# Layer 0 router weights: stored transposed in DRAM and spread over the rows of an expert pair by a DMA

## The chip, the core and the metric

The kernel runs on one core of a Trainium2 chip, as one launch. The metric is the device time in microseconds (us) of the whole launch. Five engines work side by side: TensorE (PE, with its weight loads as PEld), VectorE (DVE), ScalarE (ACT), GpSimd (POOL) and SyncE (SP), and DMA transfers are issued by an engine's queue and land later.

## The reference, cut to what matters

Two layers follow each other; each computes `x = x + s * silu(ffn(xn))`, where `s` is a recurrence (layer 0) or attention (layer 1). The change is in the mixture of experts of layer 0, with 64 experts of width 64, of which a token uses 8:

```python
def _gate(x, gate_w, gate_bias):                 # x: 4096 tokens x 128
    scores = jax.nn.sigmoid(x @ gate_w.T)
    ...                                          # best 4 of 8 groups, then best 8 experts
    tw = tw / (tw.sum(-1, keepdims=True) + 1e-20)
    return (tidx, tw * SCALE)
...
w_dense = jnp.zeros((T, E), tw.dtype).at[jnp.arange(T)[:, None], tidx].add(tw)
def body(acc, ws):
    wg, wu, wdn, cw = ws
    hmid = jax.nn.silu(x @ wg) * (x @ wu)
    return (acc + cw[:, None] * (hmid @ wdn), None)
```

The kernel computes all 64 experts for every token and multiplies the hidden values of each by its router weight `cw`, which is zero for the experts not chosen.

## The kernel before

Layer 0 (`layer0`) works on 8 tiles of 512 tokens (`NT` = 8, `TOK` = 512). Two pieces of work run beside each other for each tile `t`.

The first is the recurrence, on DVE: 32 steps of nine chained instructions (`step`, L756 to L771). Between the steps stand, at fixed places, pieces of the next tile's preparation (`between`): its layer norm at steps 3, 6, 7 and 12, its router (`route`, L643 to L697) after step 20, the key sums and coefficients of its recurrence at steps 23 to 27 (`coefficients`, the last one L726), and at steps 5 and 9 the output norm of the tile before (`out_sums`, L776, and `out_norm`, L780).

The second is the experts, in 32 pairs and one shared expert (`PAIRS + 1` = 33 rounds), a pipeline over three engines with the two experts of a pair side by side on the 128 partitions, 64 rows each:

- PE (`experts`) fills slots of a ring of four PSUM banks: the gate product and the up product of a pair (`split3`, L502 to L504), and as third slot the router weights of the pair, spread over its 128 rows by a product of a selector matrix `sel` with the transposed weights `cwt` (L583). It then does the down product of the pair two back (`down`, L554).
- ACT (`tile`, L481) copies each slot to SBUF, into the rings `act_g`, `act_u` and `act_c` of three pairs each. Before a pair's first copy it waits until the pair three back has been used (`s_h`).
- POOL (`tile`) multiplies `act_g` and `act_u` (L387) and then with `act_c` (L391), for the shared expert only once (L394). PE's down product takes the result.

At a tile's start PE transposes the router weights (L545) and ACT copies them to `cwt` (L459). At its end ACT copies the sum (L483), PE transposes it (L591), ACT applies silu (L485), and SP stores the gate to `g_scratch` (L267). At the top of pair 15 PE and ACT project the next tile (`project`); SP stores the result in 16 transfers to `z_scratch` (L260) and loads it back (L263). ACT takes it up at pair 22 (`recurrence_inputs`), POOL at pair 23 (`products`) and pair 29 (`vectors`, L327 to L340, which waits for the coefficients of DVE, L726). At pair 5 POOL does the gating of the recurrence's output of the tile before (`gated`, L345 to L352), which waits for the end of its 32 steps on DVE; DVE's `out_sums` at step 5 waits for it. SP stores the finished output at L271. Every order is written out by hand, and each engine executes its program in that order. Layer 1 starts when layer 0 is done.

The rows of the first tile's weights pass through the three rings as staging buffers; POOL splits them (L367, L369), and ACT's slots begin after the last split (`s_split`). All DMAs of the kernel before are issued by SP.

Of the kernel before, what the change touches and what calls it, by code (L numbers as in the profile page):

```python
# [7 lines left out]
F32 = mybir.dt.float32  # L8
# [6 lines left out]
P = 128  # L15
# [3 lines left out]
TOK = B * TP  # L19
# [18 lines left out]
NEG = -1e30  # L38
SLOTS = 3 * PAIRS + 2
STEPS = 9  # L40
# [20 lines left out]
def layer0(nc, d, scratch, sem):  # L61

    z_dram, y_dram, g_dram = scratch
    with ExitStack() as ctx:
# [4 lines left out]
        ident = sb("ident", [P, P])  # L69
        onehot = sb("onehot", [P, E0])  # L70
        tri = sb("tri", [P, G0 * G0])
# [12 lines left out]
        wd = sb("wd", [P, PAIRS + 1, D])  # L84
        sel = sb("sel", [P, E0, F0], F32R)
        x_sb = sb("x_sb", [P, NS, D])
# [16 lines left out]
        cw_sum = sb("cw_sum", [P, NS])  # L103
        cws = sb("cws", [P, NS, 2 * E0], F32R)
        cwt = sb("cwt", [P, TOK], F32R)
        RING = 3
        act_g = sb("act_g", [P, RING, TOK])
        act_u = sb("act_u", [P, RING, TOK])
        act_c = sb("act_c", [P, RING, TOK])
        hid1 = sb("hid1", [P, TOK])  # L110
# [25 lines left out]
        s_eps = sem("eps_set")  # L136
        s_sel = sem("selectors_ready")
        s_w1t_ps = sem("transposed_small_in_psum")
# [21 lines left out]
        s_rt = sem("router_chain")  # L160
        s_cws = sem("router_weights_split")
        s_cwt_ps = sem("router_weightsT_in_psum")
        s_cwt = sem("router_weightsT_ready")
        s_slot = sem("moe_slot_filled")
        s_ev = sem("moe_slot_copied")
# [22 lines left out]

        LN, PREP, POST, ROUTE = 3, 7, 4, 57
        RAW, WHOLE = 5, 14  # L190
# [15 lines left out]
        root, neg_beta, am_scale, square, along_k, q_am = (coef[:, i, :] for i in range(6))  # L206
        SMALL = 13

# [8 lines left out]
        def _(sp):  # L217
# [86 lines left out]
        def _(pool):  # L304
# [66 lines left out]
            def tile(t, par, first, ahead):  # L371
                for p in range(PAIRS + 1):
                    if not first and p == POST_PAIRS[0]:
                        gated(t - 1, 1 - par)
                    if not first and p == POST_PAIRS[1]:
                        normed(t - 1)
                    if ahead and p == PREP_PAIRS[0]:
                        products(t + 1, 1 - par)
                    if ahead and p == PREP_PAIRS[1]:
                        vectors(t + 1, 1 - par)  # L380

                    pool.wait_ge(s_ev, t * SLOTS + min(3 * p + 3, SLOTS))
                    g, u, c = act_g[:, p % RING, :], act_u[:, p % RING, :], act_c[:, p % RING, :]
# [21 lines left out]
        def _(act):  # L405
# [50 lines left out]
            def tile(t, par, first, ahead):  # L456

                act.wait_ge(s_cwt_ps, t + 1)
                act.activation(cwt[:, :], pb[:, 1, :], ACT.Copy).then_inc(s_cwt, 1)  # L459

                act.wait_ge(s_gst, t * 16)
                act.wait_ge(s_split, len(chunks) + 1)
                for r in range(SLOTS):
                    p, what = r // 3, r % 3
# [3 lines left out]
                    if ahead and r == 3 * PROJECT_PAIR:  # L468
# [30 lines left out]
        def _(pe):  # L499
# [38 lines left out]
            def experts(t, par, ahead):  # L538
                pe.wait_ge(s_cws, t + 1)
                pe.wait_ge(s_ev, t * SLOTS)  # L540
# [7 lines left out]
                pe.wait_ge(s_sel, 1)  # L548
                pe.wait_ge(s_wd, 32)
# [13 lines left out]
                for p in range(PAIRS + 1):  # L563
                    if ahead and p == PROJECT_PAIR:
                        pe.wait_ge(s_ev, t * SLOTS + 3 * p)
                        project(t + 1, 1 - par)
                        pe.wait_ge(s_zc, (t + 2) * NS)
                        pe.wait_ge(s_sc, t + 2)
                    pe.wait_ge(s_split, 2 * (2 * p // CH + 1))
                    for what, (w_hi, w_lo) in enumerate(((wg_hi, wg_lo), (wu_hi, wu_lo))):  # L570
                        r = 3 * p + what
                        slot_free(r)
# [29 lines left out]
        def _(dve):  # L602
# [37 lines left out]
            def route(t):  # L640
# [51 lines left out]
                dve.wait_ge(s_rt, c.next())  # L692
                dve.tensor_tensor(cw[:, :, :], cw[:, :, :], over(cw_sum[:, :], E0), ALU.mult).then_inc(s_rt, 1)
                dve.wait_ge(s_rt, c.next())
                dve.tensor_copy(cws[:, :, 0:E0], cw[:, :, :]).then_inc(s_rt, 1)
                dve.wait_ge(s_rt, c.next())
                dve.tensor_tensor(cws[:, :, E0:2 * E0], cw[:, :, :], cws[:, :, 0:E0].bitcast(F32), ALU.subtract).then_inc(s_cws, 1)  # L697
                c.check()
# [972 lines left out]
def build(nc, d, out):  # L1671
# [3 lines left out]

    z = scratch("z_scratch", NT, NS, BS, H0, TP, ZC)
    y = scratch("y_scratch", NT, P, TP, HD0)
    g0 = scratch("g0_scratch", NT, NS, P, D)
    x2 = scratch("x2_scratch", B, N, D)
    g1 = scratch("g1_scratch", B, N, D)  # L1680
    with ExitStack() as ctx:
        def sem(name):
            return ctx.enter_context(nc.semaphore(name))

        layer0(nc, d, (z, y, g0), sem)
        layer1(nc, d, (y, g0, x2, g1), out, sem)


def constants():
# [3 lines left out]
        "c_ident": np.eye(P, dtype=f),  # L1693
        "c_onehot": np.tile(np.eye(E0, dtype=f), (2, 1)),
        "c_tri": np.tril(np.ones((G0, G0), f), -1).reshape(-1),
# [48 lines left out]
```

## Time and profile before

| | |
|---|---|
| time, median of 3 runs | 2396.91 us (2391.91 to 2397.82) |
| profiled execution, its time | 2401.08 us |
| its span | 2399.3 us |
| mean granted TensorE clock | 0.882 of full speed |
| layer 0: experts' first slot copy, last store of the recurrence's output | 100.67 us, 1323.12 us |
| busy: PE, DVE, ACT, POOL | 77%, 67%, 45%, 38% of the span |

The times in the profile are counted from the start of the span. Layer 0 takes its first 1323 us, layer 1 the rest. A share of busy time is an average over both layers.

### The profile page before, as it was taken

The page shows a single profiled execution, that of the slowest core. Times are in us where ns is not written, and L with a number is a line of the kernel's source. Part 1 is how long each engine was busy: PE and PEld are TensorE (multiplying, and loading weights), DVE is VectorE, ACT ScalarE, POOL GpSimd, SP SyncE. Part 2 cuts the span into 40 slices and gives each one's busy share as a digit, 9 for nine tenths or more (in the row PEclk, how much of TensorE's full clock was granted, in tenths as well). Part 3 has the DMA queues.
Part 4 walks back from the last instruction along what each step waited for, and adds up shares of the span by engine and source line. Part 5 has one row for each costly group of instructions (what it writes and reads, how often), then busy time and mean ns, then how long its engine had stood idle before and what let it go on. Part 6 is the DMA issues. An engine that isn't in the chain of part 4 may idle for free. (4 is left out here: it accounts for less than half of the span.)

```text
span 2399.3 us, 35571 instructions
## 1 busy us (share of the span) xinstructions
PE 1837.1 (77%) x10242; PEld 1372.1 (57%) x10242; DVE 1615.1 (67%) x4233; ACT 1075.5 (45%) x1779; POOL 910.0 (38%) x729
## 2 busy tenths in 40 slices
PE   1384875866848768477486299898999999999998
PEld 1252553533525435244253288787888777777776
DVE  3599899898997989989989344444444444444443
ACT  2262553643625536355253155454455344444443
POOL 2776775757767667577486100000000000000000
PEclk8697887977978879789798599999999799999999
DMA  6220030200300203002000411111100100000000
GB/s 108 59 49 0 10 49 6 38 17 6 54 1 14 45 6 54 0 5 49 5 5 5 118 21 22 23 23 24 19 14 14 40 8 14 13 13 13 13 13 11
DMA packets 140839, 60.21 MB, mean 25 GB/s; under 512 B 94599, under 2 KB 135036, under 8 KB 140668
## 3 DMA queue, kind: packets, MB, share of 16 engines
q1 hardware_dynamic: 140668, 58.24, 12.0%
q8 instruction: 70, 1.15, 0.2%
q14 instruction: 101, 0.83, 0.1%
HBM read 37.10 MB, written 21.10 MB: 24 GB/s over the span
## 5 line engine op out<-in xcount | busy, mean ns | idle before, releaser
L554 PE MATMUL pb<-hid,wd 128*128 128x512 f32 x528 | 319.8, 691 | 215.6 <-POOL hid L391 211.0
L387 POOL TENSOR_TENSOR hid<-act_g,act_u 128x512 f32<-128x512 f32 x256 | 331.1, 1293 | 277.4 <-ACT act_c L481 260.1
L391 POOL TENSOR_TENSOR hid<-hid,act_c 128x512 f32<-128x512 f32 x256 | 332.7, 1300 | 20.1
L481 ACT ACTIVATE act_g<-pb 128x512 f32<-128x512 f32 (+1 forms) x264 | 158.5, 600 | 389.2 <-PE pb L504 386.1
L1239 PE MATMUL l_pb<-l_xt,l_big 128*128 128x512 f32 (+1 forms) x1024 | 299.4, 415 | 34.6 <-DVE l_rope L1518 24.1
L1586 DVE SCALAR_TENSOR_TENSOR l_acc<-l_pb,l_gtok,l_acc 128x128 f32<-128x128 f32 x512 | 144.0, 344 | 256.8 <-PE l_pb L1239 256.8
L502 PE MATMUL pb<-xt_hi,wg_hi 128*128 128x512 f32 (+1 forms) x264 | 223.9, 848 | 67.0 <-DMA wd<-in_L_ffn_Ws_down_dram 51.1
L554 PEld LDWEIGHTS pb<-hid,wd 128*128 128x128 f32 x528 | 96.6, 208 | 301.6 <-POOL hid L391 280.1
L1239 PEld LDWEIGHTS l_pb<-l_big,l_hid 128*128 128x128 f32 x2048 | 247.1, 192 | 10.6
L1628 DVE TENSOR_REDUCE l_mrow<-l_pb 128x2 f32<-128x256 f32 (+1 forms) x256 | 137.2, 556 | 171.9 <-PE l_pb L1239 168.9
L1167 ACT ACTIVATE l_hid<-l_pb,l_cols 128x512 f32<-128x512 f32 x256 | 169.4, 688 | 183.1 <-PE l_pb L1239 182.7
L1239 PE MATMUL l_pb<-l_big,l_hid 128*128 128x128 f32 x2048 | 247.9, 275 | 0.0
L1239 PEld LDWEIGHTS l_pb<-l_xt,l_big 128*128 128x128 f32 x1024 | 194.6, 200 | 73.0 <-DVE l_rope L1518 22.7
L756 DVE TENSOR_TENSOR products<-zr,rs 128x512 f32<-128x512 f32 x256 | 175.7, 686 | 23.7 <-POOL zr L340 10.4
L1204 ACT ACTIVATE l_big<-l_pb 128x768 f32<-128x768 f32 x128 | 104.6, 817 | 176.0 <-PE l_pb L1398 89.4
L502 PE MATMUL pb<-xt_hi,wu_hi 128*128 128x512 f32 (+1 forms) x264 | 116.3, 441 | 77.8 <-ACT act_g L481 77.7
L759 DVE TENSOR_REDUCE rs<-products 128x32 f32<-128x512 f32 x256 | 175.8, 687 | 0.0
L1105 POOL TENSOR_TENSOR l_ql<-l_rope,l_qh 128x512 f32 x8 | 10.3, 1289 | 434.5 <-ACT l_qh L1161 434.5
L757 DVE TENSOR_TENSOR products<-zr,rs 128x512 f32<-128x512 f32 x256 | 174.1, 680 | 0.0
L481 ACT ACTIVATE act_u<-pb 128x512 f32<-128x512 f32 (+1 forms) x264 | 158.1, 599 | 24.6 <-PE pb L504 16.5
L481 ACT ACTIVATE act_c<-pb 128x512 f32<-128x512 f32 x256 | 153.1, 598 | 0.0
L1239 PE MATMUL l_pb<-l_mT,l_esel 128*128 128x256 f32 x512 | 143.3, 280 | 0.0
(305 smaller groups left out, 4125.4 us busy)
## 6 DMA issues: line engine op xcount, KB each, us to landing
z_scratch<-zs SPq DMA_DIRECT2D x128, 81.0 KB, 4.2
zr<-z_scratch SPq DMA_DIRECT2D x8, 1296.0 KB, 8.4
x_sb<-in_L_attn_x_dram SPq DMA_DIRECT2D x32, 64.0 KB, 3.2
g_scratch<-act_u SPq DMA_DIRECT2D x8, 256.0 KB, 2.3
y_scratch<-yo SPq DMA_DIRECT2D x8, 256.0 KB, 2.3
l_xs<-in_L_attn_x_dram SPq DMA_DIRECT2D x32, 64.0 KB, 1.9
l_ys<-y_scratch SPq DMA_DIRECT2D x128, 16.0 KB, 1.7
l_gs<-g_scratch SPq DMA_DIRECT2D x8, 256.0 KB, 3.0
```

The lines of the kernel that those rows point to most:

```text
L387: pool.tensor_tensor(hid1[:, :], g, u, ALU.mult).then_inc(s_h1, 1)
L391: pool.tensor_tensor(hid[:, p % 2, :], hid1[:, :], c, ALU.mult).then_inc(s_h, 1)
L481: act.activation(dst, pb[0:n, r % 4, :], ACT.Silu if what == 0 else ACT.Copy).then_inc(s_ev, 1)
L502: pe.matmul(out, l_hi, r_hi, start=first, stop=False, skip_group_check=True)
L554: last = pe.matmul(pb[:, 4, :], wd[0:n, p, :], hid[0:n, p % 2, :], start=(p == 0), stop=(p == PAIRS), skip_group_check=True)
L756: dve.tensor_tensor(products[:, 2:4], two(ZG), twice, ALU.mult).then_inc(s_st, 1)
L757: dve.tensor_tensor(products[:, 0:2], two(ZF), twice, ALU.mult).then_inc(s_st, 1)
L759: dve.tensor_reduce(rs[:, 3, 0:2], products[:, 2:4], AX.X, ALU.add).then_inc(s_st, 1)
L1167: act.activation(hid[:, r % HR, :], pb[:, 2 + r % 3, :], ACT.Relu, bias=cols[:, r:r + 1]).then_inc(s_hid, 1)
L1239: return pe.matmul(out, l, r, start=start, stop=stop, skip_group_check=True)
L1586: dve.scalar_tensor_tensor(out=acc[:, s, :], in0=pb[:, 5 + e % 2, sub], scalar=gtok[par][:, s, e:e + 1], in1=acc[:, s, :], op0=ALU.mult, o ...
L1628: dve.tensor_reduce(mrow[:, k, 2 * j:2 * j + 2], src, AX.X, ALU.max).then_inc(s_ua_dve, 1)
```

## The change

Instead of a third PSUM slot for each pair, the transposed router weights go to DRAM once per tile (`c_scratch`, 64 experts x 512 tokens, two copies in turn), and for each pair a DMA issued by ACT reads the two experts' rows of it, each 64 times, into the 128 rows of `act_c`. It is issued two pairs ahead. The ring of `act_c` grows from three pairs to five. The weights are no longer split in two parts on DVE, the selector matrix and its constant are gone, and PE's transposition takes the unsplit weights. A pair now has two slots instead of three; the places of the other work, which are counted in slots, are renumbered so that they stay at the same pairs.

```diff
-SLOTS = 3 * PAIRS + 2
+SLOTS = 2 * PAIRS + 2
...
-        cws = sb("cws", [P, NS, 2 * E0], F32R)
-        cwt = sb("cwt", [P, TOK], F32R)
-        RING = 3
+        cwt = sb("cwt", [E0, TOK])
+        RING, CRING = 3, 5
...
-        act_c = sb("act_c", [P, RING, TOK])
+        act_c = sb("act_c", [P, CRING, TOK])
...
-        PROJECT_PAIR, NORM_SLOT, INPUT_SLOT = 15, 24, 66
-        POST_SLOT, KEY_SLOT = 30, 84
+        PROJECT_PAIR, NORM_SLOT, INPUT_SLOT = 15, 16, 44
+        POST_SLOT, KEY_SLOT = 20, 56
...
+        def spread(t, p):
+            per_tile = len(range(p % CRING, PAIRS, CRING))
+            return s_c[p % CRING], (t * per_tile + p // CRING + 1) * 16
...
-            sp.dma_start(onehot[:, :], d["c_onehot"]).then_inc(s_small, 16)
...
-                    pool.wait_ge(s_ev, t * SLOTS + min(3 * p + 3, SLOTS))
+                    pool.wait_ge(s_ev, t * SLOTS + 2 * p + 2)
...
                         pool.wait_ge(s_h1, t * PAIRS + (p + 1))
+                        pool.wait_ge(*spread(t, p))
...
-                act.activation(cwt[:, :], pb[:, 1, :], ACT.Copy).then_inc(s_cwt, 1)
+                act.activation(cwt[:, :], pb[0:E0, 1, :], ACT.Copy).then_inc(s_cwt, 1)
+
+                def load_weights(p):
+                    src = c_dram[par, 2 * p:2 * p + 2, :].unsqueeze(1).to_broadcast([2, F0, TOK])
+                    act.dma_start(act_c[:, p % CRING, :], src).then_inc(s_c[p % CRING], 16)
 
                 act.wait_ge(s_gst, t * 16)
                 act.wait_ge(s_split, len(chunks) + 1)
+                act.wait_ge(s_cwt, t + 1)
+                act.dma_start(c_dram[par], cwt[:, :]).then_inc(s_cst, 16)
+                act.wait_ge(s_cst, (t + 1) * 16)
+                load_weights(0)
+                load_weights(1)
...
                     if what == 0 and p >= RING:
                         act.wait_ge(s_h, t * (PAIRS + 1) + (p - RING + 1))
-                    dst = (act_g, act_u, act_c)[what][0:n, p % RING, :]
+                    if what == 0 and p + 2 < PAIRS:
+                        load_weights(p + 2)
+                    dst = (act_g, act_u)[what][0:n, p % RING, :]
...
-                    last = pe.transpose(pb[:, 1, P * s:P * (s + 1)], cws[:, s, :].bitcast(F32), ident[:, :])
+                    last = pe.matmul(pb[0:E0, 1, P * s:P * (s + 1)], cw[:, s, :], ident[:, :], start=(s == 0), stop=True, skip_group_check=True)
...
-                    if p < PAIRS:
-                        r = 3 * p + 2
-                        slot_free(r)
-                        pe.matmul(pb[:, r % 4, :], sel[:, 2 * p:2 * p + 2, :].rearrange("p a b -> p (a b)"), cwt[:, :], start=True, stop=True).then_inc(s_slot, 1)
...
-            dve.tensor_copy(sel[:, :, :], over(onehot[:, :], F0)).then_inc(s_sel, 1)
...
-                dve.tensor_copy(cws[:, :, 0:E0], cw[:, :, :]).then_inc(s_rt, 1)
-                dve.wait_ge(s_rt, c.next())
-                dve.tensor_tensor(cws[:, :, E0:2 * E0], cw[:, :, :], cws[:, :, 0:E0].bitcast(F32), ALU.subtract).then_inc(s_cws, 1)
...
+    c = scratch("c_scratch", 2, E0, TOK)
```

## Rows read from the trace of the kernel before

**Rows 1.** The page: busy us, share and instructions of each engine.

```profile
PE 1837.1 (77%) x10242; PEld 1372.1 (57%) x10242; DVE 1615.1 (67%) x4233; ACT 1075.5 (45%) x1779; POOL 910.0 (38%) x729
```

**Rows 2.** Waits up to 1400 us: who waited for whom, total, times, longest.

```profile
POOL zr L327 <- DVE coef L726: 72.5, 8, 9.9
DVE ynorm L776 <- POOL prod L352: 68.9, 8, 11.9
```

**Rows 3.** Timeline of POOL, PE, ACT and DVE around the change of tile.

```profile
694.90 0.20 DVE L726 TENSOR_TENSOR coef<-sums,coef 128x32 f32<-128x32 f32 x1
...
708.10 2.08 PE L554 MATMUL pb<-hid,wd 128*128 128x512 f32 x2 [18.05 <-POOL hid L391]
...
712.19 1.27 POOL L391 TENSOR_TENSOR hid<-hid,act_c 128x512 f32<-128x512 f32 x1
...
712.53 1.06 PE L554 MATMUL pb<-hid,wd 128*128 128x512 f32 x1
...
714.28 1.26 POOL L394 TENSOR_TENSOR hid<-act_g,act_u 64x512 f32<-64x512 f32 x1 [0.82 <-PE pb L554]
...
722.39 0.60 ACT L459 ACTIVATE cwt<-pb 128x512 fp32r<-128x512 f32 x1 [3.70 <-PE pb L545]
...
727.17 1.30 POOL L387 TENSOR_TENSOR hid<-act_g,act_u 128x512 f32<-128x512 f32 x1 [11.63 <-ACT act_c L481]
728.54 1.30 POOL L391 TENSOR_TENSOR hid<-hid,act_c 128x512 f32<-128x512 f32 x1
...
739.47 1.30 POOL L391 TENSOR_TENSOR hid<-hid,act_c 128x512 f32<-128x512 f32 x1
...
745.61 0.69 DVE L776 TENSOR_REDUCE ynorm<-prod 128x32 f32<-128x512 f32 x1 [11.93 <-POOL prod L352]
```

**Rows 4.** Timeline of DVE at the end of a tile's router.

```profile
663.69 1.24 DVE L695 CAST cws<-cw 128x256 fp32r<-128x256 f32 x1
664.96 1.44 DVE L697 TENSOR_TENSOR cws<-cw,cws 128x256 fp32r<-128x256 f32 x1
```

**Rows 5.** The instructions on line 583 and on line 481 to act_c.

```profile
L583 PE MATMUL pb<-cwt,sel x256: 388/397/632, 101.6 to 1289.8; 128*128 128x512 f32 x128
...
L481 ACT ACTIVATE act_c<-pb x256: 590/592/646, 102.9 to 1290.5; 128x512 f32<-128x512 f32 x128
```

**Rows 6.** DMA in 1339.8:1340.3, 453:454.2, 719.5:721.2, 91:97: packets, MB, busy share of 16 engines.

```profile
q1 hardware_dynamic: 2, 0.00, 0.2%
...
q1 hardware_dynamic: 144, 0.26, 58.2%
...
q1 hardware_dynamic: 528, 0.26, 48.2%
...
q1 hardware_dynamic: 880, 1.80, 104.2%
```

**Rows 7.** Timeline of ACT around a projection: the last copy before, the first work after.

```profile
613.84 0.59 ACT L481 ACTIVATE act_c<-pb 128x512 f32<-128x512 f32 x1
...
627.70 1.28 ACT L481 ACT_TABLE_LOAD   x1 [1.25 <-PE pb L504]
```

**Rows 8.** DMA issues: KB each, median us from issue to landing.

```profile
z_scratch<-zs SPq DMA_DIRECT2D x128, 81.0 KB, 4.2
...
g_scratch<-act_u SPq DMA_DIRECT2D x8, 256.0 KB, 2.3
```

**Rows 9.** Two stretches: length, busy PE PEld DVE ACT POOL, clock, DMA share, GB/s.

```profile
563.56:721.26 157.70, 110.24 (x344) 69.13 (x345) 148.36 (x387) 76.62 (x127) 106.87 (x84) 0.82 0.13 25
...
1193.96:1298.80 104.84, 95.12 (x296) 55.57 (x296) 92.58 (x227) 58.09 (x103) 90.19 (x71) 0.94 0.02 6
```

**Rows 10.** Timeline: the last split of the expert weights; the last stores of layer 0.

```profile
95.23 0.32 POOL L369 TENSOR_TENSOR wu_lo<-act_c,wu_hi 128x64 fp32r<-128x64 f32 x1
...
1319.45 1.04 POOL L352 TENSOR_TENSOR prod<-yo 128x512 f32<-128x512 f32 x1
...
1323.12 0.34 SPq L271 DMA_DIRECT2D y_scratch<-yo  x1
```

More of the change, by code:

```diff
@@ L61, in layer0 @@
 def layer0(nc, d, scratch, sem):
-    z_dram, y_dram, g_dram = scratch
+    z_dram, c_dram, y_dram, g_dram = scratch
     with ExitStack() as ctx:
@@ L69, in layer0 @@
         ident = sb("ident", [P, P])
-        onehot = sb("onehot", [P, E0])
         tri = sb("tri", [P, G0 * G0])
@@ L84, in layer0 @@
         wd = sb("wd", [P, PAIRS + 1, D])
-        sel = sb("sel", [P, E0, F0], F32R)
         x_sb = sb("x_sb", [P, NS, D])
@@ L136, in layer0 @@
         s_eps = sem("eps_set")
-        s_sel = sem("selectors_ready")
         s_w1t_ps = sem("transposed_small_in_psum")
@@ L160, in layer0 @@
         s_rt = sem("router_chain")
-        s_cws = sem("router_weights_split")
+        s_cw = sem("router_weights_ready")
         s_cwt_ps = sem("router_weightsT_in_psum")
         s_cwt = sem("router_weightsT_ready")
+        s_cst = sem("router_weightsT_stored")
+        s_c = [sem(f"router_weights_spread{i}") for i in range(CRING)]
         s_slot = sem("moe_slot_filled")
@@ L187, in layer0 @@
         s_yst = sem("y_stored")
-        LN, PREP, POST, ROUTE = 3, 7, 4, 57
+        LN, PREP, POST, ROUTE = 3, 7, 4, 55
         RAW, WHOLE = 5, 14
@@ L206, in layer0 @@
         root, neg_beta, am_scale, square, along_k, q_am = (coef[:, i, :] for i in range(6))
-        SMALL = 13
+        SMALL = 12
+        def spread(t, p):
+            per_tile = len(range(p % CRING, PAIRS, CRING))
+            return s_c[p % CRING], (t * per_tile + p // CRING + 1) * 16
         stages = [r[:, 0:2, :].rearrange("p a b -> p (a b)") for r in (act_g, act_u, act_c)]
@@ L380, in tile @@
                         vectors(t + 1, 1 - par)
-                    pool.wait_ge(s_ev, t * SLOTS + min(3 * p + 3, SLOTS))
-                    g, u, c = act_g[:, p % RING, :], act_u[:, p % RING, :], act_c[:, p % RING, :]
+                    pool.wait_ge(s_ev, t * SLOTS + 2 * p + 2)
+                    g, u, c = act_g[:, p % RING, :], act_u[:, p % RING, :], act_c[:, p % CRING, :]
                     if p < PAIRS:
@@ L458, in tile @@
                 act.wait_ge(s_cwt_ps, t + 1)
-                act.activation(cwt[:, :], pb[:, 1, :], ACT.Copy).then_inc(s_cwt, 1)
+                act.activation(cwt[:, :], pb[0:E0, 1, :], ACT.Copy).then_inc(s_cwt, 1)
+                def load_weights(p):
+                    src = c_dram[par, 2 * p:2 * p + 2, :].unsqueeze(1).to_broadcast([2, F0, TOK])
+                    act.dma_start(act_c[:, p % CRING, :], src).then_inc(s_c[p % CRING], 16)
                 act.wait_ge(s_gst, t * 16)
                 act.wait_ge(s_split, len(chunks) + 1)
+                act.wait_ge(s_cwt, t + 1)
[3 more added lines that the diff above has]
+                load_weights(1)
                 for r in range(SLOTS):
-                    p, what = r // 3, r % 3
+                    p, what = r // 2, r % 2
                     n = P if p < PAIRS else F0
@@ L467, in tile @@
                         norm(t + 1)
-                    if ahead and r == 3 * PROJECT_PAIR:
+                    if ahead and r == 2 * PROJECT_PAIR:
                         project(t + 1, 1 - par)
@@ L538, in experts @@
             def experts(t, par, ahead):
-                pe.wait_ge(s_cws, t + 1)
+                pe.wait_ge(s_cw, t + 1)
                 pe.wait_ge(s_ev, t * SLOTS)
@@ L544, in experts @@
                 for s in range(NS):
-                    last = pe.transpose(pb[:, 1, P * s:P * (s + 1)], cws[:, s, :].bitcast(F32), ident[:, :])
+                    last = pe.matmul(pb[0:E0, 1, P * s:P * (s + 1)], cw[:, s, :], ident[:, :], start=(s == 0), stop=True, skip_group_check=True)
                 last.then_inc(s_cwt_ps, 1)
                 pe.wait_ge(s_cwt, t + 1)
-                pe.wait_ge(s_sel, 1)
                 pe.wait_ge(s_wd, 32)
@@ L564, in experts @@
                     if ahead and p == PROJECT_PAIR:
-                        pe.wait_ge(s_ev, t * SLOTS + 3 * p)
+                        pe.wait_ge(s_ev, t * SLOTS + 2 * p)
                         project(t + 1, 1 - par)
@@ L570, in experts @@
                     for what, (w_hi, w_lo) in enumerate(((wg_hi, wg_lo), (wu_hi, wu_lo))):
-                        r = 3 * p + what
+                        r = 2 * p + what
                         slot_free(r)
@@ L692, in route @@
                 dve.wait_ge(s_rt, c.next())
-                dve.tensor_tensor(cw[:, :, :], cw[:, :, :], over(cw_sum[:, :], E0), ALU.mult).then_inc(s_rt, 1)
-                dve.wait_ge(s_rt, c.next())
-                dve.tensor_copy(cws[:, :, 0:E0], cw[:, :, :]).then_inc(s_rt, 1)
-                dve.wait_ge(s_rt, c.next())
-                dve.tensor_tensor(cws[:, :, E0:2 * E0], cw[:, :, :], cws[:, :, 0:E0].bitcast(F32), ALU.subtract).then_inc(s_cws, 1)
+                dve.tensor_tensor(cw[:, :, :], cw[:, :, :], over(cw_sum[:, :], E0), ALU.mult).then_inc(s_cw, 1)
                 c.check()
@@ L1683, in sem @@
             return ctx.enter_context(nc.semaphore(name))
-        layer0(nc, d, (z, y, g0), sem)
+        layer0(nc, d, (z, c, y, g0), sem)
         layer1(nc, d, (y, g0, x2, g1), out, sem)
@@ L1693, in constants @@
         "c_ident": np.eye(P, dtype=f),
-        "c_onehot": np.tile(np.eye(E0, dtype=f), (2, 1)),
         "c_tri": np.tril(np.ones((G0, G0), f), -1).reshape(-1),
```

## The prediction

> **What bounds the kernel now.** I read the page first. DVE is busy 67% of the span and no engine is full [rows 1], which says little, since two layers of different kinds are averaged. The page's chain that ended last lies in layer 1 only, so layer 0 has to be read from its waits. There two engines wait for each other [rows 2]: POOL waits 72.5 us in 8 times for DVE's last coefficient (L726), and DVE waits 68.9 us in 8 times for the gating (L352). The timeline shows one turn of that loop [rows 3]: coefficient at 694.90, POOL's vectors and its last pairs, the last hidden product at 714.28, the turn of the tile on PE and ACT (`cwt` copied by 722.99), POOL's first pair at 727.17, its fifth by 740.77, the gating, and DVE goes on at 745.61 after 11.93 us of idling. So what sets a tile of 157.70 us [rows 9] is a loop: about 50.7 us from L726 to L776 on POOL, and DVE's own steps and router for the rest. Between pair 6 and pair 28 the experts have slack: POOL arrives about 9 us early at the coefficient (72.5 / 8). POOL's own pace is 2.73 us a pair, (739.47 − 728.54) / 4 [rows 3].
>
> **What the change removes.** (a) ACT's copy of `act_c`, 0.59 us x 256, and PE's selector product, 0.40 us x 256 [rows 5]. They go in pairs where POOL's 2.73 us is the longer, so I cost them at nothing: POOL's products cover them. If POOL were not the cover, 0.6 us a pair would be the most. (b) On DVE the two instructions L695 and L697, from 663.69 to 666.40, 2.7 us a tile [rows 4]. They lie in the loop, and are worth 19 us over the seven tiles that have a next one, so long as the loop stays the bound. (c) The selector's setup at the start: under it DVE also waits for products that ACT and PE make, so nothing.
>
> **What it adds at a tile's start.** After the copy to `cwt` ACT stores it, waits for the landing, and issues loads 0 and 1 before its first slot copy. By the gate store, 2.3 us to landing [rows 8], and about 0.4 us for an issue, an estimate from L271's 0.34 us [rows 10], the first weights land 0.4 + 2.3 + 0.4 + 2.3 = 5.4 us after `cwt`, if a load takes what that store took. Before, POOL needed them 728.54 − 722.99 = 5.55 us after it [rows 3]. ACT is free 0.4 + 2.3 + 0.8 = 3.5 us after it, and POOL's first product needs two copies more, 1.2 us: 4.7 us, where it was 727.17 − 722.99 = 4.2 us. So POOL starts about 0.6 us later. Below is 0, above are two landings of 4.2 us, as of the z stores [rows 8].
>
> **What it adds for each pair, the term that decides.** A load of 256 KB as 128 packets of 2 KB. The trace has such a packet: the output store in 453:454.2 is 128 data packets and 16 small ones, busy 58.2% of 16 engines for 1.2 us: 11.2 us of engine time, 87 ns each [rows 6]. Over 16 engines that is 0.7 us, hidden without trace. Over how many engines does this one go? The 16 small packets are completions, one per engine: the gate store too has 512 + 16 = 528. The single-row load of `bkv` in 1339.8:1340.3 is 2 packets, one of data and one completion, thus one engine [rows 6]. Its outermost count is one; the stores that use 16 have 128. The other transfers of before go over 16, 32 or more rows; none has an outermost count of 2. The spread's source is `[2, F0, TOK]`: two experts outside, 64 repetitions inside. That the trace leaves open; the ends are one engine and 16. A transfer shared out along its outermost index can be cut into two parts here, and of the rows the single-row load is the nearer (2 against 1, not 2 against 128). I take two engines, each with 64 packets. One engine would be 128 x 87 ns = 11.1 us a pair; I give it no share, as the outer index has two values to share out.
>
> The Trainium skill (DMA: Bandwidth & Descriptors, section "Why a DMA increments its semaphore by 16 and not by 1") says that a transfer is split along each side's slowest dimension that is not 1, over the largest number up to 16 that divides both, and that the lowest-numbered engines are taken; its "Rules for kernel authors" name a small outermost dimension as what confines a DMA. By that rule it is 2, always the same two engines, and the single-row load agrees with it (one engine); by the 128-row stores alone it would be 16. This rule speaks against the change.
>
> **The price with two engines.** 64 x 87 ns = 5.57 us a pair, 178.2 us a tile, against 2.73 us of POOL. The packets of the weight load in 91:97, where all engines are full, take 1.042 x 6 x 16 / 880 = 114 ns [rows 6]: 7.3 us a pair, 233 us a tile. Two engines alone load the memory little, so I take 87 and keep 114 for the range. Loading two pairs ahead in program order does not help: five buffers hide latency, not a pace. PE, at its slowest, needs 4.4 us for a down product and six others (708.10 to 712.53 [rows 3]), less than 5.57, and the projection holds ACT for 13.3 us (614.43 to 627.70 [rows 7]) while four loads (22 us) are outstanding; so the two engines stay fed inside a tile. The rest of layer 0's transfers also use these two: DMA share 0.13 of 157.70, 20.5 us per engine and tile, in the last tile 0.02 of 104.84, 2 us [rows 9]. They come on top (below: 0, if they fell in the gaps). At a tile's end the queue runs dry: from the last pair's L391 at 712.19 to `cwt` at 722.99 10.8 us [rows 3], store issue and landing 0.4 + 2.3, and 1.5 us until the next packets (2.3 us less the gate store's 0.482 x 1.7 = 0.8 us of packets [rows 6, 8]): 15.0 us.
>
> **The sum.** First packets: last split over at 95.55 [rows 10], plus 0.4 + 2.3 + 1.5 = 99.8. Last packet: 99.8 + 8 x 178.2 + 7 x 20.5 + 2 + 7 x 15.0 = 1776. Then L391, the wait for PE and L394, 3.4 us; the gating, 4.6 us (740.77 to 745.6 without its overlap) and 2.6 us from L352's end to the store at 1323.12 [rows 10]: 1787. Before it was 1323.1, so +463 us. The savings (a) and (b) are void: DVE and POOL wait for the weights. Layer 1 is untouched. From the profiled execution's own 2401.1 that is 2864, and the median of the runs is 4 us under it: **2860 us**. What is late next: z stores share their two slow engines with the spread, and so ACT's inputs at pair 22 may wait; behind them on ACT stand the load issues, and 5 loads in flight (28 us) cover it.
>
> No step of this rests on SP's queue; ACT's gains 33 issues a tile, some 13 us at 0.4 us, in an engine busy 76.62 of 157.70 us [rows 9].
>
> **Rivals.**
> - Faster: the load runs on 16 engines. Then it is hidden, (b) gives −19 us, the start costs 0.6 x 8 = +5: 2397 − 14 = 2383 us. For it: 128 destination rows, like the two stores that use 16. Against: the source's two. It decides from four engines on: 32 packets x 87 ns = 2.78 us, POOL's pace.
> - No change: 16 engines, but the chain of store, wait and load costs what z transfers do, 2 x 4.2 + 0.8 = 9.2 us, 3.7 more than the 5.55 there were. In seven tiles 7 x (3.7 − 2.7) = +7 us: 2404. It turns from gain to loss where the chain passes 8.3 us.
> - Much slower: two engines and 114 ns, for instance because 64 reads of one row of DRAM do not run as the store does: 8 x 54.8 = +438: 3298 us.
>
> The Trainium skill (the same page, "Issuing engines are not separate DMA queues") states that transfers issued by ACT and by SP share the same engines. No run here shows it yet; by it the 146 us of other traffic in the sum stand, without it they go.
>
> **How the numbers follow.** Two engines near 87 ns 0.72, two slow ones 0.17, 16 engines and faster 0.07, 16 engines and no change 0.04. Hence slower 0.89, faster 0.07, same 0.04, where 0.3% (7 us) is about what a measurement of this kernel can tell from no change. The range begins where the other traffic adds nothing, 2860 − 146 = 2714, and ends at the slow packet, 3298: 2710 to 3300. It leaves out the two small cases and some of the tails.
>
> **What would show it.** Right: each spread 5 to 6 us or more in packets, DMA share in layer 0 near 2/16 plus the old, POOL's L391 waiting for a DMA in most pairs, tiles of some 214 us, DVE far under full, a lower granted clock. Also one completion packet per engine: 2 for a spread. Wrong: 16 completions, POOL at 2.7 us a pair, and tiles of about 155 us. The likeliest way to be wrong inside the mechanism is the packet's duration: each 10 ns of it makes 164 us (8 x 32 x 64 x 10 ns).

## The result and the profile after

The changed kernel takes 2768.8 us (median of 4 runs, 2765.9 to 2774.5) against 2394.8 us (4 runs): a ratio of 1.1565, with a 95% interval of 1.154 to 1.159. Forecast were 2860 us, between 2710 and 3300. The profiled execution took 2769.66 us, its span is 2767.9 us.

The page of the changed kernel: the busy row that answers to [rows 1], the granted clock and the DMA share in 40 slices, and the two hardware queues (packets, MB, share of 16 engines).

```profile
PE 1948.4 (70%) x10018; PEld 1380.3 (50%) x10018; DVE 1554.5 (56%) x4216; ACT 931.0 (34%) x1523; POOL 896.8 (32%) x729
...
PEclk7687786777878877777777885999999989999999
DMA  5222121131131131131121113111111010000000
...
q1 hardware_dynamic: 140524, 58.20, 9.2%
q10 hardware_dynamic: 33920, 68.16, 6.7%
```

DVE, ACT and POOL are less busy than before. PE is busier, at a lower clock (0.84 on average, against 0.882): it has less to do, 10018 instructions against 10242, and takes longer for each. Queue q10 is new, and holds ACT's transfers alone. Its packets can be counted out: 256 loads of 128 data packets, 8 stores of `cwt` of 64, and 16 completions for a store. 33920 − 8 x (64 + 16) = 33280 = 256 x 130, so a load has **two** completions, one for each engine it runs on.

The waits of the stretch up to 1700 us, which answer to [rows 2] (who waited for whom, total, times, longest).

```profile
ACT act_g L495 <- issue: 814.0, 184, 12.1
...
POOL hid L389 <- ACT act_u L495: 506.9, 175, 14.4
...
DVE ynorm L780 <- POOL prod L354: 217.8, 8, 43.4
POOL hid L394 <- DMA act_c<-c_scratch: 171.9, 124, 7.9
```

I had said that POOL would wait for a DMA in most pairs. It does so in 124 of 256, a little under half, and the largest wait stands elsewhere: ACT waits 814 us "for issue", for nothing that the profile shows but its own queue. The timeline shows how both are one thing (start, duration, engine, line, operation, idle time before it and its releaser).

```profile
697.45 0.59 ACT L462 ACTIVATE cwt<-pb 64x512 f32<-64x512 f32 x1 [2.05 <-PE pb L559]
...
699.42 0.53 ACTq L471 DMA_DIRECT2D c_scratch<-cwt  x1
...
701.74 3.55 ACTq L466 DMA_DIRECT2D act_c<-c_scratch  x3
705.33 0.60 ACT L495 ACTIVATE act_g<-pb 128x512 f32<-128x512 f32 x1 [7.29 <-issue]
...
705.52 5.38 ACTq L466 DMA_DIRECT2D act_c<-c_scratch  x1
...
709.37 1.27 POOL L394 TENSOR_TENSOR hid<-hid,act_c 128x512 f32<-128x512 f32 x1 [1.59 <-DMA act_c<-c_scratch]
714.77 1.26 POOL L394 TENSOR_TENSOR hid<-hid,act_c 128x512 f32<-128x512 f32 x1 [1.30 <-DMA act_c<-c_scratch]
720.07 1.26 POOL L394 TENSOR_TENSOR hid<-hid,act_c 128x512 f32<-128x512 f32 x1 [2.69 <-DMA act_c<-c_scratch]
725.46 1.26 POOL L394 TENSOR_TENSOR hid<-hid,act_c 128x512 f32<-128x512 f32 x1 [0.89 <-DMA act_c<-c_scratch]
730.81 1.26 POOL L394 TENSOR_TENSOR hid<-hid,act_c 128x512 f32<-128x512 f32 x1 [0.97 <-DMA act_c<-c_scratch]
```

POOL's second product comes every (730.81 − 714.77) / 3 = 5.35 us, where it came every 2.73 us [rows 3]; so a packet of 2 KB takes 5.35 / 64 = 83.6 ns. And a single issue holds ACT for 5.38 us, about the time of one load (the next ones take 3.44, 7.14 and then 4.96 us each): with about three loads outstanding the next issue goes in only as an earlier one drains. That this wait follows from the pace, and isn't a second cause, is argued here and tested by e3.

Two stretches, from the copy to `cwt` to the next one and from the last such copy to the last pair, as in [rows 9] (length, busy PE PEld DVE ACT POOL, clock, DMA share, GB/s), and the DMA view of 740 to 770 us (packets, MB, share of 16 engines).

```profile
697.45:898.35 200.90, 117.04 (x316) 65.48 (x316) 137.22 (x372) 58.80 (x96) 104.47 (x84) 0.80 0.19 59
1499.93:1680.20 180.27, 109.61 (x260) 58.79 (x260) 110.21 (x270) 39.13 (x70) 86.97 (x69) 0.81 0.13 50
```

```profile
q10 hardware_dynamic: 730, 1.47, 13.0%
```

13.0% of 16 engines is 2.1 engines: two are full, the other fourteen all but idle. A tile takes 200.9 us instead of 157.7.

### The profile page after: what moved, and what is told of

It reads as the page before. It is cut to its first block and busy times, and to the rows that moved or that the text cites. A ratio compares the mean times of both kernels' runs of the same rounds, so it can differ in the third digit from the quotient of the medians.

```text
span 2767.9 us, 34798 instructions
## 1 busy us (share of the span) xinstructions
PE 1948.4 (70%) x10018; PEld 1380.3 (50%) x10018; DVE 1554.5 (56%) x4216; ACT 931.0 (34%) x1523; POOL 896.8 (32%) x729
## 3 DMA queue, kind: packets, MB, share of 16 engines
q10 hardware_dynamic: 33920, 68.16, 6.7%
## 5 line engine op out<-in xcount | busy, mean ns | idle before, releaser
L567 PE MATMUL pb<-hid,wd 128*128 128x512 f32 x528 | 381.9, 814 | 462.5 <-POOL hid L394 456.0
L495 ACT ACTIVATE act_g<-pb 128x512 f32<-128x512 f32 (+1 forms) x264 | 157.7, 597 | 971.7 <-issue 814.0
L394 POOL TENSOR_TENSOR hid<-hid,act_c 128x512 f32<-128x512 f32 x256 | 324.9, 1269 | 247.4 <-DMA act_c<-c_scratch 171.9
L567 PEld LDWEIGHTS pb<-hid,wd 128*128 128x128 f32 x528 | 103.0, 234 | 590.5 <-POOL hid L394 573.7
L516 PEld LDWEIGHTS pb<-xt_hi,wg_hi 128*128 128x128 f32 (+1 forms) x264 | 63.1, 239 | 299.3 <-ACT act_g L495 153.8
L760 DVE TENSOR_TENSOR products<-zr,rs 128x512 f32<-128x512 f32 x256 | 175.7, 686 | 23.7 <-POOL zr L342 10.4
L495 ACT ACTIVATE act_u<-pb 128x512 f32<-128x512 f32 (+1 forms) x264 | 156.6, 593 | 4.6 <-PE pb L518 4.4
L517 PE MATMUL pb<-xt_lo,wg_hi 128*128 128x512 f32 (+1 forms) x264 | 131.4, 498 | 0.0
## 6 DMA issues: line engine op xcount, KB each, us to landing
zr<-z_scratch SPq DMA_DIRECT2D x8, 1296.0 KB, 11.3
```

The costliest lines, as they stand in the source:

```text
L516: pe.matmul(out, l_hi, r_hi, start=first, stop=False, skip_group_check=True)
L567: last = pe.matmul(pb[:, 4, :], wd[0:n, p, :], hid[0:n, p % 2, :], start=(p == 0), stop=(p == PAIRS), skip_group_check=True)
L760: dve.tensor_tensor(products[:, 2:4], two(ZG), twice, ALU.mult).then_inc(s_st, 1)
```

## The experiments

**Two transfers (e1).** Each pair's load is cut into two, one for each expert, with an outermost count of 64. The bytes, packets and buffers stay.

```diff
-                    src = c_dram[par, 2 * p:2 * p + 2, :].unsqueeze(1).to_broadcast([2, F0, TOK])
-                    act.dma_start(act_c[:, p % CRING, :], src).then_inc(s_c[p % CRING], 16)
+                    for a in range(2):
+                        src = c_dram[par, 2 * p + a:2 * p + a + 1, :].to_broadcast([F0, TOK])
+                        act.dma_start(act_c[F0 * a:F0 * (a + 1), p % CRING, :], src).then_inc(s_c[p % CRING], 16)
```

> The spread of a pair is issued as two transfers, one per expert, each with 64 repetitions of one row as its outermost dimension; bytes, packets and order of work are those of the changed kernel. If the outermost count of 2 confines the transfer to two engines (the theory): 16 completions for each transfer, a pair's packets over in about 0.7 us, the pace back at POOL's 2.7 us, tiles of about 155 us and a time of 2375 to 2400 us. If the pace comes from reading one row of DRAM 64 times, or from the bytes, or from ACT's issue of DMAs (now twice as many): no faster than 2769 us, and slower if the issue is the cause.

**Four engines (e2).** As e1, but one transfer for a pair, with outermost count four; for this the store writes each expert's row twice.

```diff
-                act.dma_start(c_dram[par], cwt[:, :]).then_inc(s_cst, 16)
+                act.dma_start(c_dram[par], cwt[:, :].unsqueeze(1).to_broadcast([E0, 2, TOK])).then_inc(s_cst, 16)
...
+                    rows = c_dram[par, 2 * p:2 * p + 2].rearrange("e k n -> (e k) n")
+                    src = rows.unsqueeze(1).to_broadcast([4, F0 // 2, TOK])
+                    act.dma_start(act_c[:, p % CRING, :], src).then_inc(s_c[p % CRING], 16)
```

> One transfer per pair as in the changed kernel, but the router weights are stored twice beside each other in DRAM, so that the source has an outermost count of 4 (each row repeated 32 times). By the theory: 4 completions per spread, 32 packets of about 84 ns on each engine, 2.7 us a pair, which is POOL's pace, so that the tile is set by the loop of DVE and POOL again: 2385 to 2430 us. If the transfer takes two engines whatever the source, or the pace is not that of engines: about 2769 us.

**A ring of four (e3).** The changed kernel with four buffers instead of five, and the load one pair ahead: fewer loads wait in the queue.

```diff
-        RING, CRING = 3, 5
+        RING, CRING = 3, 4
...
-                load_weights(1)
...
-                    if what == 0 and p + 2 < PAIRS:
-                        load_weights(p + 2)
+                    if what == 0 and p + 1 < PAIRS:
+                        load_weights(p + 1)
```

> Still two engines, but only one pair ahead and a ring of four buffers, so that at most four loads are in flight instead of five. If the two engines' pace sets the time (the theory), nothing moves inside a tile: 2769 us, give or take 15. If ACT, which is held up in issuing loads while the queue is full, sets it, fewer loads in flight free it and the time falls by more than 30 us.

**Two transfers and DVE's split put back (e4).** As e1, with the two instructions that the change removed from DVE's router; their result is used by nothing.

```diff
-                dve.tensor_tensor(cw[:, :, :], cw[:, :, :], over(cw_sum[:, :], E0), ALU.mult).then_inc(s_cw, 1)
+                dve.tensor_tensor(cw[:, :, :], cw[:, :, :], over(cw_sum[:, :], E0), ALU.mult).then_inc(s_rt, 1)
+                dve.wait_ge(s_rt, c.next())
+                dve.tensor_copy(cws[:, :, 0:E0], cw[:, :, :]).then_inc(s_rt, 1)
+                dve.wait_ge(s_rt, c.next())
+                dve.tensor_tensor(cws[:, :, E0:2 * E0], cw[:, :, :], cws[:, :, 0:E0].bitcast(F32), ALU.subtract).then_inc(s_cw, 1)
```

> As the run with two transfers per pair, with the two DVE instructions that split the router weights put back behind the router (their result is not used). If they lie in the loop of DVE and POOL: 15 to 22 us slower than that run (2.7 us in seven tiles). If the loop is no longer the bound: no difference beyond 5 us.

Measured, all four on one chip against 2396.0 us (e3 from two executions, the others from six to ten):

| | median us | ratio (95% interval) |
|---|---|---|
| e1 two transfers | 2401.9 | 1.0022 (1.0004 to 1.0040) |
| e2 four engines | 2404.5 | 1.0031 (1.0016 to 1.0046) |
| e3 ring of four | 2759.7 | 1.1514 (1.1474 to 1.1553) |
| e4 two transfers, split | 2417.7 | 1.0089 (1.0060 to 1.0119) |

The pages of e1 and of e2, the new queue:

```profile
q10 hardware_dynamic: 41600, 68.19, 9.6%
```

```profile
q10 hardware_dynamic: 34944, 69.21, 8.1%
```

e1 has 512 x (64 + 16) + 8 x 80 = 41600 packets, e2 256 x (128 + 4) + 8 x (128 + 16) = 34944: 16 completions and 4, as many as the engines meant. The same loads on 16 or on 4 engines take the 367 us away (e1 2 us above the range that was expected, e2 inside it). That four are as good as 16 within 3 us shows that the load has only to keep POOL's pace. The Trainium skill (DMA: Bandwidth & Descriptors, section "Why a DMA increments its semaphore by 16 and not by 1") takes on each side of a transfer the slowest dimension that is not 1, and gives the transfer the largest number of engines up to 16 that divides both; 2, 4 and 16 completions for outermost counts of 2, 4 and 64 agree with it.

In e3 ACT's wait for its queue falls by 382 us, and POOL's for the load rises by 293 us, while the time falls by 9 us:

```profile
POOL hid L394 <- DMA act_c<-c_scratch: 464.6, 155, 8.6
ACT act_g L494 <- issue: 431.7, 108, 12.6
```

So the held issue is how the pace of two engines shows, not a cause beside it, for which the expectation wanted more than 30 us.

But e1 is also not faster than before, although DVE's 2.7 us a tile are gone; e4 shows that they count (15.8 us, 2.3 us a tile). Something else was added. e1's turn of a tile:

```profile
716.66 0.59 ACT L462 ACTIVATE cwt<-pb 64x512 f32<-64x512 f32 x1 [1.24 <-PE pb L560]
...
717.95 0.47 ACTq L472 DMA_DIRECT2D c_scratch<-cwt  x1
...
720.23 3.69 ACTq L467 DMA_DIRECT2D act_c<-c_scratch  x6
...
723.96 0.60 ACT L496 ACTIVATE act_g<-pb 128x512 f32<-128x512 f32 x1 [6.71 <-issue]
...
726.59 1.27 POOL L394 TENSOR_TENSOR hid<-hid,act_c 128x512 f32<-128x512 f32 x1 [0.18 <-POOL hid L389]
```

ACT stands in the way of its own copies: the store, 2.3 us to its landing, then six issues, three pairs' and not two, since pair 2 is loaded at pair 0. POOL's second product starts 9.3 us after the end of `cwt`'s copy (717.25), where it was 5.55 us [rows 3]. The issues aren't all of it: e2, with three issues of 1.71 us in their place, starts no earlier (second product 11.8 us behind the gate's silu, e1 11.9). There the store takes 3.0 us to land, with twice the bytes, and POOL waits for the loads, 37.7 us in 31 times.

**The wait behind the first copies (e5).** As e1, but ACT makes pair 0's two copies before it waits for the store and issues the first loads.

```diff
-                act.wait_ge(s_cst, (t + 1) * 16)
-                load_weights(0)
-                load_weights(1)
...
-                    if what == 0 and p + 2 < PAIRS:
+                    if r == 2:
+                        act.wait_ge(s_cst, (t + 1) * 16)
+                        for q in range(3):
+                            load_weights(q)
+                    if what == 0 and 0 < p < PAIRS - 2:
                         load_weights(p + 2)
```

> As the run with two transfers per pair, but at a tile's start ACT first makes the two copies of pair 0 and only then waits for the store of the router weights and issues the loads of pairs 0, 1 and 2. In that run POOL's second product came 9.2 to 10.4 us after the copy to cwt began, 6.1 us in the kernel before. If the loss at the tile's start is ACT waiting and issuing six DMAs ahead of its first copy: POOL's second product at about 7 us, 2 to 3 us less in each of eight tiles, 2380 to 2388 us. If the loss is the chain of store and load itself: no more than 1 us a tile, 2395 to 2402 us.

**The transposition at pair 30 (e6).** As e1, but PE transposes the next tile's weights in the tile before, into a bank of its own, ACT stores them there, and issues the first loads behind the gate's silu, without a wait at the tile's start.

```diff
+        CW_PAIR = 30
...
-        pb = ctx.enter_context(nc.psum_tensor("pb", [P, 5, 512], F32))
+        pb = ctx.enter_context(nc.psum_tensor("pb", [P, 6, 512], F32))
...
+                    if ahead and r == 2 * CW_PAIR:
+                        store_weights(t + 1, 1 - par)
...
+                if ahead:
+                    first_loads(t + 1, 1 - par)
...
+                    if ahead and p == CW_PAIR:
+                        pe.wait_ge(s_cwt, t + 1)
+                        weights_transposed(t + 1)
```

> As the run with two transfers per pair, but the router weights of the next tile are transposed, copied and stored at pair 30 of the tile before (in a PSUM bank of their own), and the loads of pairs 0 and 1 are issued right after the silu of the gate. The chain of store and load then lies wholly beside other work and the transposition leaves the loop. By the theory that the tile's start in the loop of DVE and POOL is what the variant with two transfers lost: 5 to 6 us less a tile, 2350 to 2365 us, with DVE's wait for the gating falling from about 11 us to 5. If something else holds the loop, for instance ACT's issues of two DMAs a pair: above 2390 us.

**Half rows on two engines (e7).** The changed kernel with each load as two transfers of half the row: the same bytes on the same two engines, in twice the packets.

```diff
+                    for h in (slice(0, TOK // 2), slice(TOK // 2, TOK)):
+                        src = c_dram[par, 2 * p:2 * p + 2, h].unsqueeze(1).to_broadcast([2, F0, TOK // 2])
+                        act.dma_start(act_c[:, p % CRING, h], src).then_inc(s_c[p % CRING], 16)
```

> As the changed kernel, on two engines, but each spread is cut into two transfers of half of the tokens: the same bytes in twice as many packets, of 1 KB. In the kernel before, the 1 KB packets of a weight load took a median of 46 ns. If the pace is the sum of the packets' times on an engine: 128 x 46 ns = 5.9 us a pair instead of 5.35, 2769 + 8 x 32 x 0.54 = 2907 us. If it is bytes alone: 2769 us. If there is a fixed cost per transfer: more than 2907 us.

Measured against 2399.7 us: e5 2386.8 us (ratio 0.9955, 0.9936 to 0.9974), e6 **2372.7 us** (0.9891, 0.9859 to 0.9924), e7 2970.6 us (1.2390, 1.2325 to 1.2455). e5 falls into its range; e6 beats both kernels, but by 27 us where 35 to 50 had been expected. Both confirm the start of a tile as the place where e1 had lost its gain. e7's DMA view of 700 to 740 us:

```profile
q10 hardware_dynamic: 1756, 1.77, 13.4%
```

Less the completions (27 small packets are in this window) some 1730 packets of 1 KB share two engines for 40 us: 46 ns each, where 2 KB took 83.6. That is 5.92 us a pair against 5.35, 146 us in the layer, and about what was expected; the kernel takes 202 us more. Most of the rest stands at a tile's start, where ACT now makes six issues before its first copy:

```profile
780.79 11.85 ACTq L467 DMA_DIRECT2D act_c<-c_scratch  x6
```

The changed kernel's three took 3.55 us. From the gate's silu to POOL's first product it is 18.5 us in e7 and 10.9 us there, 53 us in seven tiles. So of a packet's time neither the bytes alone nor the number of packets alone is the price, and the doubled issues cost beside it.

**The early transposition alone and with fewer engines.** e8 is e6 with e2's four-engine load, which needs half the issues, issued behind the pair's two copies (the first diff, against e6; the store writes each row twice, as in e2). e9 is the kernel before with its transposition and copy at pair 30, and nothing else.

```diff
-                for a in range(2):
-                    src = c_dram[par, 2 * p + a:2 * p + a + 1, :].to_broadcast([F0, TOK])
-                    act.dma_start(act_c[F0 * a:F0 * (a + 1), p % CRING, :], src).then_inc(s_c[p % CRING], 16)
+                rows = c_dram[par, 2 * p:2 * p + 2].rearrange("e k n -> (e k) n")
+                src = rows.unsqueeze(1).to_broadcast([4, F0 // 2, TOK])
+                act.dma_start(act_c[:, p % CRING, :], src).then_inc(s_c[p % CRING], 16)
...
-                    if what == 0 and p + 2 < PAIRS:
-                        load_weights(par, p + 2)
...
+                    if what == 1 and p + 2 < PAIRS:
+                        load_weights(par, p + 2)
```

> As the run with the early transposition, but with one transfer per pair over four engines (the weights stored twice beside each other) instead of two over 16, and a pair's load issued after its two copies instead of before. ACT's issues halve and none stands before pair 0's copies except the first two loads. In the run with the early transposition ACT issued six transfers between the silu of the gate and its first copy, 5.3 us. If these issues still hold the tile's start: 1 to 2 us less a tile, 2358 to 2368 us. If the start is held by PE or if four engines are too few for the spread beside the z traffic: 2370 us or more.

```diff
-                act.activation(cwt[:, :], pb[:, 1, :], ACT.Copy).then_inc(s_cwt, 1)
+                act.activation(cwt[:, par, :], pb[:, 5, :], ACT.Copy).then_inc(s_cwt, 1)
...
+                    if ahead and r == 3 * CW_PAIR:
+                        copy_weights(t + 1, 1 - par)
...
+                    if ahead and p == CW_PAIR:
+                        pe.wait_ge(s_cwt, t + 1)
+                        weights_transposed(t + 1)
```

> The kernel before, with nothing of the change, but with the transposition of the next tile's router weights moved to pair 30 in the same way (a PSUM bank and a second buffer of cwt). This tells what the early transposition is worth without the spread in DRAM. The loop of DVE and POOL loses about 3 us a tile between the silu of the gate and the copy to cwt (1.4 to 4.3 us in the trace) and the copy itself: 2370 to 2380 us. If it comes to the time of the run with the early transposition and two transfers (2373 us), the spread in DRAM itself is worth nothing; if it stays at 2385 us or more, the two DVE instructions that the change removes are what the rest of the gain rests on.

Measured against 2397.3 us: e8 2397.5 us (1.0005, 0.9986 to 1.0024), far from the 2358 to 2368 that fewer issues were to give; e9 2389.5 us (0.9962, 0.9937 to 0.9987), a miss too: 8 us of gain where 17 to 27 had been expected. By its expectation the two DVE instructions are then what the rest of e6's gain rests on. e8's row in the waits, and the landing times of its gate store, with those of e6 below:

```profile
ACT act_g L499 <- DMA g_scratch<-act_u: 55.8, 7, 9.1
...
DMA to landing us min/median/max: 2.3/7.5/8.8
```

```profile
DMA to landing us min/median/max: 2.3/3.3/3.6
```

`first_loads` now runs beside the gate's store, and its loads, 32 packets on each of four engines, stand with the store's shares on those engines; ACT's next `act_g` waits for the store's landing, 55.8 us in 7 times. Two loads are 64 packets on each of the four, by 87 ns 5.6 us, an estimate that fits the 5.2 us from 2.3 to 7.5. Over 16 engines the same loads leave it at 3.3 us.

**Which half of e8 missed (e10).** e8 with the load over 16 engines again; the issues stay behind the pair's two copies (the diff is against e6).

```diff
-                    if what == 0 and p + 2 < PAIRS:
-                        load_weights(par, p + 2)
...
+                    if what == 1 and p + 2 < PAIRS:
+                        load_weights(par, p + 2)
```

> As the run with the early transposition and two transfers over 16 engines per pair, with one thing more: a pair's load is issued after the pair's two copies instead of before them, so that ACT has four instead of six issues to make between the silu of the gate and its first copy. From the silu of the gate to POOL's first product it took 6.9 us in that run, 9.7 us in the run over four engines, where ACT waited for the gate store. If those two issues hold the start: 5.5 to 6 us, 1 us less a tile, 2360 to 2370 us. If the gate's store or PE holds it: the same as that run, 2373 us within 4.

Measured: 2375.8 us against 2397.8 (0.9913, 0.9886 to 0.9940), as e6 within the error. The four engines, not the issues' place, lost e8's gain. The place does shorten the start, as was expected if the two issues held it (5.8 us from the silu to the first product, e6 6.9), but the time doesn't fall with it.

One table of the loop from the timelines, means over seven tiles in us: from the gate's silu to POOL's first and second product, from the last coefficient to the gating (L726 to L776 in the kernel before), the rest of the loop, which is DVE's, the router in it (without the split; from the start of its first instruction to that of its last), and the tile.

| | silu to first | to second | coefficient to gating | DVE's part | router | tile |
|---|---|---|---|---|---|---|
| before | 7.5 | 8.8 | 49.0 | 107.9 | 17.1 | 157.1 |
| e1 | 10.4 | 11.9 | 52.2 | 104.3 | 14.8 | 156.6 |
| e2 | 9.6 | 11.8 | 51.9 | 105.3 | 15.9 | 157.2 |
| e4 | 10.5 | 12.2 | 52.6 | 107.0 | 15.5 | 159.7 |
| e5 | 5.3 | 9.4 | 50.6 | 103.8 | 15.0 | 154.2 |
| e6 | 6.9 | 8.5 | 48.6 | 104.8 | 16.1 | 153.6 |
| e9 | 6.3 | 7.7 | 48.1 | 108.2 | 17.3 | 156.7 |
| e8 | 9.7 | 11.3 | 51.2 | 106.0 | 16.3 | 157.3 |
| e10 | 5.8 | 7.4 | 47.7 | 107.0 | 18.9 | 154.9 |

What e1 loses at the start, 3.1 us a tile, is the 3.2 us by which its third column grows, and DVE's part gives 3.6 back. These are single executions, which differ by some us from the median (e1's, at 2396.5, lies 5 under its own), so the columns tell more than small differences of the last one. The router is one and the same program in e1 and e10, and takes 14.8 and 18.9 us; the last section shows why. In this execution of e10 (2383.5, 8 over its median) that takes back more than the shorter start gives.

## Why the prediction was right, point by point

The mechanism and its place came out as said; the forecast was 91 us too high.

- **Two engines.** Right: two completions a load, 2.1 engines busy, and the whole loss gone when the outermost count alone changes (e1, e2). The reading from single-row and 128-row transfers was a guess from two against one; the runs made it a fact for counts of 2, 4 and 64.
- **The packet.** 87 ns by the output store, 83.6 measured. Eight tiles of 178.2 us are eight of 5.35 x 32 = 171.2.
- **Other traffic and the dry time.** A tile was to be 178.2 + 20.5 + 15.0 = 213.7 us and is 200.9. The queue runs dry longer than said: in the turn shown the last packet ends at 685.3 us and the next begins at 703.0, 17.7 us, as the DMA views show (GB/s in 40 slices, first of 682 to 692 us, then of 701 to 706 us):

```profile
GB/s 49 49 49 49 49 49 49 25 25 25 25 25 25 0 0 0 0 0 0 0 0 0 33 0 0 0 0 0 0 0 0 0 33 0 0 0 0 0 0 33
```

```profile
GB/s 180 131 33 0 0 0 0 0 0 0 0 0 0 0 0 0 16 33 33 66 66 33 66 33 66 33 66 49 49 66 33 66 33 66 33 66 66 33 66 33
```

  There one engine ends 1.5 us before the other. What is left of the tile is 200.9 − 171.2 − 17.7 = 12.0 us, where 20.5 us stood: this is the term that was mis-sized most. Part of the other traffic falls in the dry time, when it costs nothing, which the bound "below 0" had in view but the value did not.
- **"The two engines stay fed inside a tile."** Wrong, by little. Four loads were to be outstanding over the projection, 22 us; the last issue before it ends at 781.17 us, and the queue's packets end at 795.5, 14.3 us or under three loads later:

```profile
776.24 4.93 ACTq L466 DMA_DIRECT2D act_c<-c_scratch  x1
...
794.96 0.49 ACTq L466 DMA_DIRECT2D act_c<-c_scratch  x1
```

  The next data packets begin at 798.1, so in 2.6 of the 12 us the queue moves nothing (2.0 to 2.6 us in the tiles of this trace). In most of the other 9.4 us it is slow while SP's transfers run. The first line below is 735 to 740 us; the second is 815 to 820 us, with SP's loads beside it and an issue of ACT held for 12.83 us:

```profile
q10 hardware_dynamic: 122, 0.25, 13.1%
```

```profile
q10 hardware_dynamic: 28, 0.06, 3.9%
```

  That answers what the prediction left open: SP's transfers do slow ACT's.
- **The sum.** From 7 x (213.7 − 200.9) = 90 us and 187.8 − 180.3 = 7 us in the last tile (4.2 to its first packets, 178.2, 2 and 3.4 had been said) the last store should be 97 us early. It is:

```profile
1690.04 0.34 SPq L273 DMA_DIRECT2D y_scratch<-yo  x1
```

  1787 was said, +463 us; it is +367 from 1323.12 [rows 10]. What follows it takes 2769.66 − 1690.04 = 1079.6 us, before 2401.08 − 1323.12 = 1078.0: layer 1 is untouched. Of the 97 us the packet makes 8 x 7.0 = 56 and the other traffic 7 x 8.5 = 60, and the longer dry time takes 7 x 2.7 = 19 back.
- **The savings.** Void in the changed kernel, as said. (b) was put at 19 us where the loop bounds; e4 against e1 gives 15.8 us, in the tile 3.1 us. (a), ACT's copies and PE's products, was costed at nothing. Of e6's 27 us 8 come with e9's step and 16 with (b), which leaves some 3 us for it. This is a sum over runs of different sets, and 3 us is within its error; no run isolates (a).
- **The start of a tile.** Put at +0.6 us; measured +3.4 us in the changed kernel (10.9 us from the silu to POOL's first product, before 7.5) and +3.1 us to the second in e1. The store's landing was right, 2.3 us. The step that failed is "ACT is free 0.4 + 2.3 + 0.8": I counted two issues and there are three pairs', and took 0.4 us for one where three take 3.55 us. The landing and, in e2, the load itself have their part. Beside 367 us it doesn't show, but it decides the rivals: "faster", 2383 us on 16 engines, was wrong, and "no change", 2404 us, stands beside e1's 2402, though by another wait than the one priced.
- **"It decides from four engines on."** Right at its edge: e2 2404.5 beside e1's 2401.9.
- **What is late next.** z loads land later (median 11.3 us against 8.4) but hold nobody for long. The wait I had not named is DVE's for the gating, 217.8 us instead of 68.9, with POOL itself late.

Open: the 9.4 us are what is left, not measured one by one, and no run leaves SP's transfers out. Why only three loads go into the queue ahead of the projection was not tried.

## What to carry to other kernels

Count a transfer's outermost index before its bytes: 256 KB with an outermost count of 2 took 5.35 us and set the pace of a layer; the same 256 KB with a count of 4, or as two transfers with 64, were hidden. The completions in the packet count (packets less data packets) tell from any trace how many engines a transfer used. And when a product is replaced by a store and loads, the engine that issues them pays at the start of every round: take that off the path first (e6: −27 us, of which the same step alone gives 8 us in the kernel before). What the DMA version is then worth here lies, by the sum above, in the two DVE instructions it makes needless, and hardly in the 256 copies and products.

## What the runs showed of the hardware that was not expected

- With loads of 64 packets on each of two engines outstanding, one more issue held ACT for 5.38 us, the time of a load (3.4 to 7.1 us in its neighbours); ACT's waits "for issue" are 814 us in all. A queue that is behind stops the engine that feeds it, and its compute with it.
- Half the row is not half the packet's time: 46 ns for 1 KB against 83.6 ns for 2 KB undisturbed, 10% more for the same bytes.
- A load on four of 16 engines delayed a store over all 16 from 3.3 to 7.5 us in the median, since the store has landed only when its slowest share has.
- DVE's instructions can be held by POOL's. The same instruction of the router, in the kernel before and, below, in the changed one, where POOL mostly waits (durations in ns, least, median, most):

```profile
L681 DVE TENSOR_TENSOR replaced<-replaced,masked x8: 426/1156/1170, 43.2 to 1132.6; 128x256 f32<-128x256 f32 x8
```

```profile
L689 DVE TENSOR_TENSOR replaced<-replaced,masked x8: 425/426/875, 43.2 to 1425.6; 128x256 f32<-128x256 f32 x8
```

  It is not a slower pace but a wait for the end of POOL's instruction, as two executions of it in the changed kernel show:

```profile
620.34 1.26 POOL L394 TENSOR_TENSOR hid<-hid,act_c 128x512 f32<-128x512 f32 x1 [2.02 <-DMA act_c<-c_scratch]
621.31 0.57 DVE L689 TENSOR_TENSOR replaced<-replaced,masked 128x256 f32<-128x256 f32 x1
...
822.62 1.26 POOL L394 TENSOR_TENSOR hid<-hid,act_c 128x512 f32<-128x512 f32 x1 [1.42 <-DMA act_c<-c_scratch]
823.29 0.88 DVE L689 TENSOR_TENSOR replaced<-replaced,masked 128x256 f32<-128x256 f32 x1
```

  Both end 0.28 to 0.29 us after POOL's does. The traces of the twelve kernels hold this instruction 96 times. In 74 a POOL instruction is at work when it starts, and it ends 0.28 to 0.29 us after that one, however long that takes; in the other 22, with none at work at its start, it takes 0.42 to 0.43 us. What is shared was not tried. It means that an idle POOL gives DVE some time back, and that a shorter router in one kernel is not all the change's own doing: where the router falls among POOL's instructions decides some us of it.
